# Four key blocks' value products in one run, a table of masked blocks for GpSimd, and a new order of stages, in a two-block transformer kernel on one core

## The reference

```python
x = x + tanh(g_xattn[0]) * fake_quant(layernorm(x)) @ fake_quant(ctx)
x = x + tanh(g_ffn[0]) * (layernorm(x) @ W_base.T + b_base + 0.5 * update)   # update: low-rank codes, inverse real FFT
x = x + tanh(g_xattn[1]) * attention(layernorm(x), ctx, ctx, mask)           # 32 heads of 16, 8 key/value groups
x = x + tanh(g_ffn[1]) * bitlinear(relu(bitlinear(x_n, w_gate)) ** 2 * bitlinear(x_n, w_up), w_down)
```

## Time and profile before

| What | us |
|---|---|
| median of three runs | 252.97 |
| the profiled execution | 254.72 |
| its span, first to last instruction | 252.9 |
| PE busy | 237.6 (94%) |
| DVE busy | 206.9 (82%) |
| ACT busy | 187.4 (74%) |
| POOL busy | 123.2 (49%) |

### The profile page before, as it was taken

How to read it: one execution, slowest core, us unless ns; L and a number is a source line. 1 busy time by engine, 2 the same in 40 slices (tenths; PEclk the granted TensorE clock), 3 DMA queues, 4 the chain that set the end, 5 groups by cost and what they waited for, 6 DMA issues and landing times.

```text
span 252.9 us, 4671 instructions
## 1 busy us (share of the span) xinstructions
PE 237.6 (94%) x1450; PEld 122.2 (48%) x1472; DVE 206.9 (82%) x592; ACT 187.4 (74%) x317; POOL 123.2 (49%) x177
## 2 busy tenths in 40 slices
PE   8686999999999999999999999999999999998984
PEld 8522449857543353565354375335335245443532
DVE  1788858588996696897989866989799878899995
ACT  2364696897898999685977988669789989445632
POOL 7004864634350037584786374548998786300000
PEclk9889799999999999999999999999999999999999
DMA  5999961674862930001891000900000000000004
GB/s 174 355 386 441 389 260 35 139 164 117 348 170 66 155 145 3 1 1 45 145 392 64 4 0 21 166 3 1 4 1 0 3 0 0 3 1 0 0 3 166
DMA packets 9154, 27.63 MB, mean 109 GB/s; under 512 B 1514, under 2 KB 4122, under 8 KB 7882
## 3 DMA queue, kind: packets, MB, share of 16 engines
q1 hardware_dynamic: 8698, 21.63, 29.3%
q0 software_dynamic: 288, 5.70, 5.9%
q10 hardware_dynamic: 144, 0.00, 0.0%
HBM read 23.87 MB, written 3.41 MB: 108 GB/s over the span
## 4 chain that ended last, share of the span: by engine, by line
PE 59%; DVE 14%; ACT 9%; issue 7%; POOL 4%; DMA 3%; SPq 2%; DVEq 0%; ACTq 0%; POOLq 0%
PE bank L837 10%; PE bank L809 9%; PE bank L786 8%; PE bank L812 4%; PE bank L718 4%; PE bank L860 4%; PE bank L728 4%; ACT big L1032 3%; DMA big<-in_ctx 3%; PE bank L878 3%; POOL big L594 3%; PE bank L676 2%; PE bank L897 2%; PE bank L795 2%; DVE junk L1259 1%
## 5 line engine op out<-in xcount | busy, mean ns | idle before, releaser
L1259 DVE CUSTOM_DVE_ANT_0 junk<-bank,maskb 128x512 bf16<-128x512 f32 x128 | 82.8, 686 | 12.9 <-PE bank L786 12.4
L1032 ACT ACTIVATE big<-bank 128x512 f32<-128x512 f32 x128 | 73.9, 596 | 17.2 <-PE bank L809 11.2
L594 POOL TENSOR_TENSOR big<-big,product 128x512 int32<-128x512 int32 x48 | 61.6, 1285 | 33.0 <-ACT big L1032 32.6
L809 PE MATMUL bank<-qst,kst 99*128 99x512 bf16 x128 | 48.8, 382 | 0.5
L786 PE MATMUL bank<-kst,qst 96*128 96x512 bf16 x128 | 48.3, 382 | 0.7 <-DVE mx L1259 0.4
L837 PE MATMUL bank<-big,vp 128*32 128x512 f32 x256 | 30.6, 598 | 1.0 <-POOL big L594 0.4
L604 POOL TENSOR_TENSOR mx<-mx 128x4 f32<-128x4 f32 x64 | 14.2, 223 | 23.5 <-DVE mx L1259 21.3
L812 PE MATMUL bank<-ident_b,maskb 128*128 128x512 bf16 x65 | 24.7, 380 | 0.0
L786 PEld LDWEIGHTS bank<-kst,qst 96*128 96x128 bf16 x128 | 12.7, 99 | 22.0 <-issue 10.8
L809 PEld LDWEIGHTS bank<-qst,kst 99*128 99x128 bf16 x128 | 12.4, 97 | 19.1 <-ACT big L1032 9.3
L638 POOL TENSOR_SCALAR stage_w<-stage_w,wscale 128x1376 f32<-128x1376 f32 (+1 forms) x12 | 18.4, 1542 | 5.3 <-DVE wscale L1381 5.3
(11 more groups left out here) (191 smaller groups left out, 412.5 us busy)
## 6 DMA issues: line engine op xcount, KB each, us to landing
stage_w<-in_w_down POOLq DMA_DIRECT2D x1, 2816.0 KB, 9.8
stage_w<-in_w_gate SPq DMA_DIRECT2D x1, 2752.0 KB, 15.2
stage_w<-in_w_up POOLq DMA_DIRECT2D x1, 2752.0 KB, 11.1
qst<-q_parts SPq DMA_DIRECT2D x18, 128.0 KB, 4.9
big<-in_ctxT SPq DMA_DIRECT2D x8, 256.0 KB, 15.3
q_parts<-parts SPq DMA_DIRECT2D x12, 128.0 KB
x<-in_x SPq DMA_DIRECT2D x4, 256.0 KB, 6.3
big<-in_ctx SPq DMA_DIRECT2D x4, 256.0 KB, 6.7
```

The source lines that it names most:

```text
L594: nc.gpsimd.tensor_tensor(p, p, keep[:, nt, KEEP_ST.index(i):KEEP_ST.index(i) + 1, :].broadcast_to([P, HG, P]), ALU.mult).then_inc(kept, 1)
L809: i = mm(o[:, :], kst[0:KM, b, g, s * P:(s + 1) * P], qst[0:KM, tile % 2, g * HG:(g + 1) * HG, :], start=True, stop=by_keep(c, s))
L1032: fn(pt[:, c % 4, s, :], o[:, :], ACT.Exp).then_inc(drain(stage), 1)
L1259: v.tensor_tensor_reduce(junk[:, j % 2, :], o[:, :], maskb[:, tb(c // NG)[1], :], 1.0, HIDE, ALU.add, ALU.max, mx_parts[:, c % 3, 0, hh:hh ...
```

## The change

Four things change. First, the value products of all four key blocks of a group of four chunks stand in one place, at step 28 of the group, instead of two places. Second, `by_keep` asks a table with an entry per chunk; the table names 74 blocks, spread over chunks 0 to 31, and POOL masks those, so that 54 keep the product on PE. For this there are two tiles of ones and zeros, `keep_even` for key blocks 0 and 2 and `product` for 1 and 3, and two `keepT` stages. Third, the values' stride in `vp` is 18 columns a group instead of 24, which makes room for the new tile. Fourth, `PREPARATION` and `FILL` are written in another order throughout (two of their lines are shown). In the functions below the tables, line numbers are about three lower in the new program.

```diff
-VW, VS = 32, 24
+VW, VS = 32, 18
 PREPARATION = [
-    ("load_wkv",), ("vones",), ("scalars",), ("load_x", 0), ("products",), ("xstats", 0), ("ln0", 0, 1),
+    ("fclamp", 0, 0), ("load_wkv",), ("scalars",), ("load_x", 0), ("load_adapters",), ("load_ctxT", 1), ("products",),
...
 FILL = {
-    0: [("ln2", 1, 4)], 1: [("v", 1, 2), ("ln2", 1, 5)], 2: [("fternary", 0, 1)],
+    0: [("p", 2), ("ln2", 1, 5)], 2: [("q1T", 3), ("hT", 1, 2), ("fternary", 0, 1), ("load_wo",)], 4: [("v", 1, 3)],
...
-KEEP_FROM = 8
-KEEP_ST = (0, 2)
+KEPT = "2 2 - 023 0123 0 03 23 012 02 23 02 0123 02 2 012 0123 023 013 013 012 012 23 0 012 2 013 02 123 12 012 12".split()
 
 def by_keep(c, s):
-    return c >= KEEP_FROM and s in KEEP_ST
+    return str(s) in KEPT[c]
...
-        if i >= 0 and i % 16 in (1, 3) and i // 16 < NSC:
-            s += [("pv", i // 16, i % 16 - 1), ("pv", i // 16, i % 16)]
+        if i >= 0 and i % 16 == 3 and i // 16 < NSC:
+            s += [("pv", i // 16, n) for n in range(ST)]
...
-        keep = product[:, :].bitcast(I32).rearrange("p (a s q) -> p a s q", a=SQ // P, s=len(KEEP_ST))
+        keep_even = sb("keep_even", [P, D], I32)
+        keeps = [a.rearrange("p (a s q) -> p a s q", a=SQ // P, s=2) for a in (keep_even[:, :], product[:, :].bitcast(I32))]
...
                 elif kind == "keep":
 
                     c, i = stage[1:]
-                    if KEEPS.index(stage) == 0:
-                        wait_drained(pool, ("keepT",))
+                    if stage == [k for k in KEEPS if k[2] % 2 == i % 2][0]:
+                        wait_drained(pool, ("keepT", i % 2))
                     wait_drained(pool, ("t", c, i))
...
-                    if by_keep(4 * sc + 3, s):
-                        pe.wait_ge(kept, KEEPS.index(("keep", 4 * sc + 3, s)) + 1)
-                    else:
+                    if not by_keep(4 * sc + 3, s):
                         wait_drained(pe, ("t", 4 * sc + 3, s))
+                    for c in [c for c in range(4 * sc, 4 * sc + 4) if by_keep(c, s)][-1:]:
+                        pe.wait_ge(kept, KEEPS.index(("keep", c, s)) + 1)
...
                 elif kind == "keepT":
 
                     o = wait_filled(dve, stage)[:, 0:256].bitcast(BF16)
-                    dve.wait_ge(first_added, 2 * (NT - 1))
-                    v.tensor_scalar(keep.rearrange("p a s q -> p (a s q)"), o, -1.0, 1.0, ALU.max, ALU.add).then_inc(drain(stage), 1)
+                    if t:
+                        dve.wait_ge(first_added, 2 * (NT - 1))
+                    v.tensor_scalar(keeps[t].rearrange("p a s q -> p (a s q)"), o, -1.0, 1.0, ALU.max, ALU.add).then_inc(drain(stage), 1)
```

More of the change, by code:

```diff
@@ new lines @@
+    ("load_ctx", 1), ("xstats", 0), ("ln0", 0, 1), ("ln0", 0, 2), ("ln0", 0, 3), ("warm", 0, 0, 42),
+    ("warm", 0, 1, 60), ("warm", 0, 4, 10), ("adapters",), ("load_ctx", 0), ("ln0", 0, 4), ("ln0", 0, 5),
+    ("load_ctx", 3), ("xstats", 1), ("vones",), ("cquant", 0), ("ln0q", 0), ("vt",), ("xstats", 2), ("xstats", 3),
[4 rows of a table added]
+    ("hT", 0, 1), ("load_ctxT", 5), ("mask",), ("bias", 0), ("q1T", 1), ("load_wT", 3), ("load_wT", 0),
+    ("load_mask",), ("y0", 0, 0), ("load_ctxT", 0), ("r", 1), ("load_wT", 1), ("ln0", 2, 5), ("p", 1), ("y0", 0, 1),
@@ new lines @@
+    ("y0", 0, 2), ("fabs", 0, 0), ("fabs", 0, 1), ("load_wT", 2), ("y0", 0, 3), ("fabs", 0, 2), ("fabs", 0, 3),
+    ("keepT", 0), ("k", 1, 2), ("k", 0, 2), ("load_gate",), ("load_bias",), ("load_ctxT", 2), ("v", 0, 0),
+    ("k", 0, 3), ("k", 1, 3), ("load_ctxT", 6), ("y0up", 0), ("ln2", 0, 0), ("ln2", 0, 1), ("ln2", 0, 2),
+    ("load_ctxT", 7), ("ln0q", 2), ("fsum", 0), ("load_ctxT", 3), ("v", 0, 1), ("ln2", 0, 3), ("ln2", 0, 4),
+    ("ln2", 0, 5), ("load_ones",), ("load_ctx", 4), ("load_wq",), ("ksplit", 0), ("ln1", 1, 0), ("hT", 0, 2),
[4 rows of a table added]
@@ L98 @@
+    ("y0", 1, 3), ("fternary", 0, 0), ("v", 1, 2), ("fround", 0, 1), ("fround", 0, 2), ("qpick", 0, 0),
+    ("qpick", 0, 1), ("ln0r", 3), ("r", 2), ("csum", 1), ("fround", 0, 3), ("ln2", 1, 3), ("ln2", 1, 4),
 ]
 FILL = {
[5 rows of a table removed]
-    22: [("hT", 2, 1), ("fclamp", 1, 0)], 24: [("qsplit", 1)], 25: [("fabs", 1, 0)],
-    26: [("y0", 2, 0), ("y0", 2, 1), ("y0", 2, 2), ("y0", 2, 3), ("fclamp", 1, 1), ("fabs", 1, 1), ("fabs", 1, 2)],
-    28: [("fabs", 1, 3), ("y0up", 2), ("ln2", 2, 0), ("ln2", 2, 1), ("ln2", 2, 2), ("ln2", 2, 3), ("ln2", 2, 4),
-        ("fsum", 1)],
@@ L132 @@
-    114: [("gu", 0, 2, 0)], 116: [("oT", 5)], 118: [("aT", 2, 1), ("ffactors", 0)], 119: [("gu", 0, 2, 1)],
-    120: [("hidden", 0, 2), ("fq", 0, 0)], 121: [("fclamp", 2, 2), ("fclamp", 2, 3), ("fternary", 2, 1)],
[18 rows of a table removed]
+    0: [("p", 2), ("ln2", 1, 5)], 2: [("q1T", 3), ("hT", 1, 2), ("fternary", 0, 1), ("load_wo",)], 4: [("v", 1, 3)],
+    6: [("vcopy", 1), ("q", 1, 0)], 7: [("q", 1, 1), ("fclamp", 0, 1), ("ksplit", 1), ("fclamp", 0, 2)],
[5 rows of a table added]
+        ("ln2", 2, 4), ("fabs", 1, 0), ("fabs", 1, 1), ("ln2", 2, 5), ("fabs", 1, 2)],
@@ new lines @@
+    27: [("ln1", 3, 0), ("ln1", 3, 1)], 28: [("ln1", 3, 2), ("hT", 2, 2), ("ln1", 3, 3)],
+    30: [("q", 2, 0), ("q", 2, 1), ("fabs", 1, 3), ("fsum", 1), ("q", 2, 2)], 31: [("fclamp", 0, 3)],
+    32: [("fround", 1, 0)], 33: [("fscale", 1)], 34: [("oT", 0)], 35: [("fclamp", 1, 0)], 36: [("fround", 1, 1)],
[3 rows of a table added]
+    51: [("bias", 3), ("fclamp", 1, 1)], 53: [("fclamp", 1, 2)], 54: [("y0", 3, 0)],
[9 rows of a table added]
+    94: [("gu", 0, 0, 1), ("fscale", 2)], 97: [("fround", 2, 0)], 98: [("oT", 4)], 99: [("hidden", 0, 0)],
@@ L152 @@
+    101: [("ln3", 1, 4)], 102: [("gu", 0, 1, 0), ("gu", 0, 1, 1)], 104: [("fround", 2, 1)],
+    106: [("gu", 0, 2, 0), ("fternary", 2, 0), ("fround", 2, 2)],
[3 rows of a table added]
+    122: [("ffactors", 0), ("aT", 2, 1), ("fternary", 2, 2), ("fternary", 2, 3)],
[17 rows of a table added]
 }
@@ L593, in _ @@
                     nt = c // NG % (SQ // P)
[L594 removed]
+                    nc.gpsimd.tensor_tensor(p, p, keeps[i % 2][:, nt, i // 2:i // 2 + 1, :].broadcast_to([P, HG, P]),
                                             ALU.mult).then_inc(kept, 1)
@@ L819, in _ @@
                     for n in range(SQ // P):
-                        for i, st in enumerate(KEEP_ST):
-                            k = len(KEEP_ST) * n + i
+                        for i, st in enumerate((t, t + 2)):
+                            k = 2 * n + i
                             last = tr(o[:, k * P:(k + 1) * P], maskb[:, n, st * P:(st + 1) * P], ident_b[:, 0, :])
```

16 lines of the change are left out of this document (removed), and 94 rows, old and new, of tables (FILL, PREPARATION).

## The result

The changed kernel takes 251.25 us (median of 15 runs, 250.41 to 253.19), the kernel before 253.65 us beside it (15 runs, 252.70 to 255.23). The ratio is 0.990, with a 95% interval from 0.988 to 0.993: 1.0% faster, where 2.4% (247 us) had been forecast. The time lies in the forecast's range, but less than half of the gain came. The profiled execution took 251.52 us, with a span of 249.7 us (before: 252.9).

The account below looks back on a forecast made before the run. PE was taken to bound nearly the whole attention loop. From the profiled 254.7 us, 254.7 - 5.7 - 1.6 + 0.2 + 3.0 - 1.5 - 0.5 = 248.6, a median of 247 us, 2.4% faster; range 243 to 252.5 us.

Parts of the forecast that it names:

- Loads that move: Output weights' load and second feed-forward weight's load stand later in their queues; put at nothing, DMA engines having bandwidth to spare.
- DVE beside POOL: In the loop, DVE passes held by POOL's instructions, 1.1 us a hit; three or four hits expected, costing nothing before the seventh.
- The 19 passes that were counted: DVE passes in the loop that POOL could hold: 11 over whole rows and 8 that read two tiles of SBUF.
- POOL's new work: 26 more masks on POOL, 33.4 us, raise PE's idle time in the loop: +3.0 us, with ends 0 and +9.
- Masks and merge: In the loop, 26 mask products leave PE, -5.7 us; 7 groups' value products merge into one run each, -1.6 us.
- ACT's wait for a merged run: ACT's exponentials wait for later value products of blocks 0 and 1: put at nothing; without cover, PE waits 4 us.
- Order ahead of the loop: Before the loop, `vt` first, `we` next, keys last: less waiting and low clock, -1.5 us, between -4 and +3.
- The end: After the last value run, PE has 0.8 us less to do: -0.5 us, between -2 and +2.
- The sum: All terms added to the profiled 254.7 us give 248.6; the median of timed runs put at 247 us.
- None of the four: Rivals: DVE becomes the bound (0.16), POOL's queue becomes the path (0.09), the start loses (0.10), more than the sum (0.07).
- the first: Rival: in the loop, DVE held beside POOL becomes the bound and PE waits for score banks; 251 us, chance 0.16.
- The second: Rival: in the loop, POOL's ordered queue of masks and maximum splits becomes the path; 259 us, chance 0.09.

Follow-up runs that it names:

- the probe: Kernel without the computation (copies x to the output): POOL masks, with or without a load's issue, beside DVE passes; newton steps without issue held 1.2 us at most.
- load_later: The changed kernel with POOL's issue of the last feed-forward weight's load at step 63 instead of 59; 244.90 us, ratio 0.966 to the kernel before.
- scenes 1 and 6: Parts of the probe: two-tensor newton steps beside 6 and 12 POOL masks, no load's issue; each step waits for one mask's end, 1.2 us at most.
- newton_scalar: The changed kernel with its three one-column newton steps written as tensor_scalar, the second tensor as scalar pointer; 246.18 us, ratio 0.970 to the kernel before.
- newton_old_masks: newton_scalar with the 48 blocks of before masked on POOL instead of 74, runs still merged; 250.90 us, ratio 0.990 to the kernel before.
- newton_split_old: newton_scalar with both 48 blocks masked on POOL and value products split into two runs; 258.30 us, ratio 1.018 to the kernel before.
- The mended kernels: The changed kernel with newton steps by scalar pointer, the load's issue later, both, or one added POOL wait behind the issue; 244.90 to 246.18 us.

## Why the prediction was wrong, step by step

- **Loads that move: nothing.** This is the step that failed. It looked at bandwidth alone, and at two loads; the last feed-forward weight's load, which moved by one step, is not in it. The issue now stands next to a newton step (the issue in step 59, the held step in 60; before, in 58 and 66) and has 5.2 us of POOL's work without a pause behind it. That cost 6.1 us. In the kernel before POOL paused 3.0 us behind the issue, and no newton step stood between; POOL and DVE there:

```profile
125.32 0.60 POOL L631 DMA_DIRECT2D stage_w<-in_w_down  x1 [1.39 <-ACT ternary L1010]
...
129.69 1.27 POOL L594 TENSOR_TENSOR big<-big,product 128x512 int32<-128x512 int32 x1 [0.82 <-ACT big L1032]
...
129.99 0.99 DVE L1108 SCALAR_TENSOR_TENSOR newton_post<-newton_post 128x1 f32<-128x1 f32 x1
```

- **DVE beside POOL: a hit is 1.1 us at most, and seven are needed.** True for a POOL without an issue (1.2 us at most for a newton step in the probe), and the other hits show no cost: load_later keeps them and has the lowest ratio. But one hit behind an issue had no such bound: 5.39 us, and it decided alone. The row that the bound came from the earlier trace rows holds no issue. The 19 passes that were counted leave out the newton steps, of which one was held for 0.99 us in the kernel before too (129.99 us, above), and among the row passes of that kernel more than one was hit: `hq` (L1305) took 1.30 us twice beside a mask, where 0.43 is its shortest. The Trainium skill's "SBUF — State Buffer", section SBUF: two separate sides, says that of a VectorE pass with two SBUF inputs and a GpSimd instruction that reads SBUF, whichever starts first has the shared ports for its whole instruction and the other blocks; by that the step would have waited some 1.2 us, as in scenes 1 and 6. Behind an issue the measurement differs: six and twelve instructions.
- **POOL's new work: +3.0.** Too high for merged runs. The 26 masks move PE's idle time little there: 1.8 of 145 us with 74 masks (newton_scalar, above), 1.5 of 150 us with 48 (newton_old_masks):

```profile
65.00:215.00 150.00, 148.47 (x908) 70.43 (x925) 127.50 (x381) 128.60 (x222) 92.91 (x124) 1.00 0.26 68
```

With split runs the term would have been too low: 10.0 of 157 us with 74 masks, 5.4 of 159 with 48 (newton_split_old). POOL's waits for exponentials and maxima fell from 48.9 to 15.5 + 4.9 = 20.4 us, as said.

- **Masks and merge: -5.7 and -1.6.** The counts and durations came as said (54 weight loads of the mask line, 74 masks, runs of 3.57 us). But their worth is not theirs alone: in this order the merge is worth 7 to 11 us, in the old one it costs 11. The paragraph that gave ACT's wait for a merged run nothing, and 4 us without cover, was about right for the new order (ACT waits 2.6 us in newton_scalar, and PE waits for no exponential there) and too low for the old one.
- **Order ahead of the loop: -1.5.** `vt` starts at 13.9 us and `we` at 20.1, with 3.60 us for its eight products; the first score product comes at 53.8 instead of 54.8 us, so 1.0 us was won. The low clock is not gone: `we` is rid of it, but `vt` takes 3.68 us for the records that took 1.94, and the mean clock of the first 30 us is 0.89 as before. The part was not run alone.
- **The end: -0.5.** 0.2 us was won (36.7 us from the last value run on, 37.0 before).
- **The sum.** The mended kernels take 244.9 to 246.2 us, just below the forecast of 247 us. That nearness is luck: two errors in the sum cancel. The order without the other parts (and with the other newton form) costs 5 us (258.3 against 253.1), where -1.8 was put, and merge and masks together give 12, where -4.3 was put.
- **The rivals.** None of the four came. DVE did become the bound, as in the first, but for 5 us at one place; its busy time in the loop grew by 6.5 us, 5.2 of them the one hold. The second, POOL's queue as the path, is in part what the new order meets with split runs (PE's value products wait 4.6 us for POOL there).

## What to carry to other kernels

Price a moved DMA issue on POOL's queue by what stands behind it there: look for a pause soon after it, and for DVE passes before that pause. A short wait on POOL behind the issue, or scalar pointers in small steps, took the hold away here at no cost that the runs show. A term read off one run of products (0.23 us a merge) is no price of moving them: with the other engines' work around it, the merge came to 11 us lost in one order of stages and 11 won in another.

## What the runs showed of the hardware that was not expected

- After a software DMA issue on POOL, a DVE pass of one column with two tensors of SBUF, or of whole rows by pointers, waits until POOL first pauses: 7.78 us behind 6 masks, 14.97 behind 12, 4.01 with a pause of 0.08 us after the third. Without the issue it waits for one instruction (1.2 us at most for the column, 1.47 us for the pass over whole rows, its own 0.55 included).
- The effect outlasts the issue: a step that starts 1.4 us behind its end is held too (7.20 us).
- A pass that multiplies two tensors of 128x512 is not held so; with an issue ahead or without, it and the masks take turns, at most 1.64 and 1.73 us for a pass and 1.71 for a mask (0.69 and 1.26 alone). Why these passes differ stays open.
